# Graph attention on one core: an extra exponential placed ahead of ScalarE's block loop in each of the three attention layers

## The chip, the cores and the metric

One core of a Trainium2 chip runs the whole program in one launch. The metric is the device time of one execution in microseconds (us). The engines are TensorE (PE; PEld are its weight loads), VectorE (DVE), ScalarE (ACT), GpSimd (POOL) and the sync engine (SP); "ACTq" in a row is an instruction that ScalarE's queue issues itself, here a DMA.

## The reference, cut to what matters

Two blocks work on a graph of 3125 nodes and 53125 edges: a dot-product attention over the edges (8 heads), a mixture of experts, two graph-attention layers (4 heads), and a small gated network. All three attention layers need, for each destination node, a softmax over its neighbours:

```python
s = jnp.einsum('edh,edh->eh', q[rows], k[cols])          # attention layer
e = jnp.exp(s - m[rows])
out = segment_sum(e / z[rows] * v[cols], rows)

e = leaky_relu(alpha_s[src] + alpha_d[dst], 0.2)         # graph-attention layer, two of them
ex = jnp.exp(e - m[dst])
out = segment_sum(h[src] * (ex / segment_sum(ex, dst)[dst]), dst)
h = gelu(out + b)
```

Nothing of this changes.

## The kernel before

`program` runs its stages one after another: the edge lists are loaded and sorted into tables of neighbours, then come the attention layer (`attend`, named att, with `qk=True`), the experts, and the two graph-attention layers (`attend`, named gt0 and gt1, with `qk=False`; their tiles are called gt_... in the profile), and `finish`.

`attend` handles destination nodes in tiles of 128. The neighbours of a tile are taken in chunks, 4 rounds (one neighbour per node and round) to a chunk; four chunks, one for each of four buffer slots, make a block. A block is one turn of a hardware loop on each engine. There are 19 turns with 4 rounds (`Fori(0, full)`, the full turns) and then 9 turns with 3 rounds (`Fori(full, blocks)`, the tail turns).

- POOL (`gather_block`, L1004 to L1009) waits until a slot's last contents have been weighted and its list of indices is there, then issues 4 (in the tail 3) indirect DMAs that gather the neighbours' rows into the slot.
- DVE (`block_of`) works on slot k and the slots before it in turn: scores (L1059 or L1061, L1069 or L1071), the running maximum (L1077), the shift by it (L1082), then for slot k-1 the weighting of the gathered rows by the exponentials (`weight_chunk`, L1088 for gt, L1092 for att), and the rescaling and adding of sums (L1101, L1107).
- ACT (`weigh_block`) computes the exponential of each slot's shifted scores (L1208). In att it also weights part of the rows with 16 short copies a slot (8 in the tail, L1213), and SP hands the slots over. In gt ACT does the handing over (`hand_over`, L1192 to L1194): it waits until the gather into the slot has landed, tells DVE, reads the next list column into a register (L947) and issues the DMA of the next indices (L944). At the end of a turn it issues the load of the next list (L951).
- PE (`sum_block`, L1259) sums the weighted rows.

In a gt turn ACT's program order is: hand over slots 0 and 1, exponential of slot 0, hand over slot 2, exponential of slot 1, and so on:

```python
for k in range(SLOTS):
    if handing and k + 1 < SLOTS:
        hand_over(k + 1, at, passed)
    n = act.snap(i * SLOTS + (k + 1))
    act.wait_ge(shifted, n)
    act.activation(wv[...] if qk else exps_of(k)[...], score[:, k, 0:rounds + 1, :], ACT.Exp).then_inc(exped, 1)
```

ScalarE evaluates functions from a table, which an `ACT_TABLE_LOAD` brings in. The compiler puts those instructions in, the kernel's source has none. It put one at the head of the first exponential in the body of each layer's loop of full turns, and none in the body of the tail loop.

Of the kernel before, what the change touches and what calls it, by code (L numbers as in the profile page):

```python
# [6 lines left out]
ALU, ACT, AX = mybir.AluOpType, mybir.ActivationFunctionType, mybir.AxisListType  # L7

P = 128
# [872 lines left out]
def attend(nc, c, g, name, heads, own, own_rows, table, width, qk, bias_row=None, begin=None, onward=None):  # L882
# [22 lines left out]
    with Mem(nc, name) as m:  # L905
# [6 lines left out]
        score = m.sb("score", [P, SLOTS, ROUNDS + 1, h])  # L912
        wv = m.sb("wv", [P, SLOTS, ROUNDS + (1 if qk else 0), h, av])
        recip = m.sb("recip", [P, 2, NT, h])
        part = m.ps("part", [P, SLOTS, 512])
        exps = None if qk else m.ps("exps", [P, SLOTS, 64])
        exps_of = lambda k: exps[:, k, 0:(ROUNDS + 1) * h].rearrange("p (r h) -> p r h", h=h)
# [17 lines left out]
        def blocks_of(eng):  # L935

            full = eng.value_load(g.counts[0:1, 0:1], min_val=MIN_FULL, max_val=MAX_FULL)
            tails = eng.value_load(g.counts[0:1, 1:2], min_val=1, max_val=TAIL_ROUNDS * NT)
            full = eng.snap((full + (SLOTS - 1)) // SLOTS)
            return full, eng.snap(full + (tails + (SLOTS - 1)) // SLOTS)  # L940

        def load_idx(eng, col, k):

            eng.dma_start(idx[:, k, :], g.neighbours[:, bass.ds(col, ROUNDS)]).then_inc(idx_in[k], 16)  # L944

        def col_of(eng, at):
            return eng.value_load(listed[0:1, bass.ds(at, 1), 1], min_val=0, max_val=MAX_COLS - ROUNDS)  # L947

        def load_list(eng, i):

            eng.dma_start(listed[:, bass.ds(i % LISTS * SLOTS, SLOTS), :], g.tile_of[bass.ds(i * SLOTS, SLOTS), :].unsqueeze(0)).then_inc(list_in, 16)  # L951

        with nc.Block(no_gpsimd_drain=True) as block:
# [228 lines left out]
            @block.scalar  # L1182
            def _(act):
                act.sem_inc(act_weighted, SLOTS)
                for k in range(groups if qk else 0):
                    part_t = slice(GROUP * k, GROUP * (k + 1))
                    act.dma_start(own[:, part_t, :], own_rows[:, part_t, 0:QW]).then_inc(own_rest if k else own_in, 16)
                    act.dma_start(acc[:, part_t, :, :].rearrange("p t h f -> p t (h f)"), own_rows[:, part_t, QW:2 * QW]).then_inc(own_rest if k else own_in, 16)
                    act.dma_start(peak[:, part_t, :], own_rows[:, part_t, 2 * QW:QX]).then_inc(own_rest if k else own_in, 16)

                def hand_over(k, at, passed):
                    act.wait_ge(gathered[k], passed)  # L1192
                    act.sem_inc(chunk_ready, 1)
                    load_idx(act, col_of(act, at + k), k)  # L1194

                def weigh_block(i, rounds, passed):
                    of_act = range(dve_rounds, rounds)
                    if handing:
                        at = act.snap((i + 1) % LISTS * SLOTS)
                        act.wait_ge(list_in, i * 16 + 32)  # L1200
                        act.sem_inc(list_seen, 1)
                        hand_over(0, at, passed)
# [5 lines that stand above are left out]
                        act.activation(wv[:, k, 0:rounds + 1, :, dh] if qk else exps_of(k)[:, 0:rounds + 1, :], score[:, k, 0:rounds + 1, :], ACT.Exp).then_inc(exped, 1)  # L1208
                        if act_rounds:
                            act.wait_ge(exped, n)  # L1210
                            for r in of_act:
                                for e in range(h):
                                    last = act.activation(wv[:, k, r + 1, e, 0:dh], rows[:, k, r, v0 + e * dh:v0 + (e + 1) * dh], ACT.Copy,  # L1213
                                                          scale=wv[:, k, r + 1, e, dh:dh + 1])
                            last.then_inc(act_weighted, 1)
                    if handing:
                        load_list(act, i + 2)

                full, blocks = blocks_of(act)
                with act.Fori(0, full) as i:  # L1220
                    weigh_block(i, ROUNDS, (i + 1) * (16 * ROUNDS))
                with act.Fori(full, blocks) as i:
                    weigh_block(i, TAIL_ROUNDS, (i + 1) * (16 * TAIL_ROUNDS) + full * (16 * (ROUNDS - TAIL_ROUNDS)))
                if handing:
                    act.wait_ge(list_in, blocks * 16 + 32)
                    act.sem_inc(list_seen, 1)
                    for k in range(SLOTS):
                        act.wait_ge(idx_in[k], blocks * 16 + 16)
                        act.sem_inc(list_seen, 1)
                def copy_group(k):  # L1230
                    for t in range(GROUP * k, GROUP * (k + 1)):
                        act.wait_ge(turned, t + 1)
                        if t >= 2:
                            act.wait_ge(projected, t - 1)
                        act.activation(a_t[:, t % 2, :, :].rearrange("p h n -> p (h n)"), part[:, t % 2, 0:D], ACT.Copy).then_inc(copied, 1)

                def gelu_group(k):
                    act.wait_ge(biased, k + 1)
                    out = own[:, GROUP * k:GROUP * (k + 1), 0:D]
                    act.activation(out, out, ACT.Gelu).then_inc(gelued, 1)  # L1240

                for k in range(0 if qk else 2 if onward is not None else groups):
                    gelu_group(k)
                for k in range(groups if onward is not None else 0):
                    copy_group(k)
                    if not qk and k + 2 < groups:
                        gelu_group(k + 2)
# [820 lines left out]
def program(nc, a, out):  # L2068
# [3 lines left out]
    with Mem(nc, "all") as m:  # L2072
# [56 lines left out]
        with Mem(nc, "first") as first:  # L2129
            wo, bo = first.sb("wo", [P, KC, D]), first.sb("bo", [P, D])  # L2130
            row_f = first.sb("row_f", [P, 2, NT])
            weights_in = first.sem("weights_in")
            loads = [(wo[:, :, :], by_half(a.Wo)), (bo[:, :], one_row(a.bo).to_broadcast([P, D])), (wr[:, :, :], by_half(a.Wr)), (br[:, :], one_row(a.br).to_broadcast([P, NE])),
                     (gw[:, :, :], by_half(a.gW)), (gb[:, :], one_row(a.gb).to_broadcast([P, E2])), (x[:, :, :], x_rows)]
            late = []
            for i, (v, s_src, s_dst) in enumerate(((a.gW0, a.a_src0, a.a_dst0), (a.gW1, a.a_src1, a.a_dst1))):
                loads.append((ga[i][:, :, 0:D], by_half(v)))
                for k, s in enumerate((s_src, s_dst)):
                    for h in range(GH):
                        late.append((vectors[i][(h % 2) * GC:(h % 2 + 1) * GC, h // 2, k * GH + h:k * GH + h + 1],  # L2140
                                     s[h, :].rearrange("(c o) -> c o", o=1)))
            with Mem(nc, "at") as p:
                own = p.sb("own", [P, NT, QW])
                attend(nc, c, graphs[0], "att", QH, own, q_ordered, kv_rows, KVP, True, begin=(loads, late, vectors, weights_in),
                       onward=(wo, own, att_rows, D, bo[:, :]))
            xn_rows = dram("xn_rows", (NPAD, D))
            add_and_norm(nc, c, att_rows, graphs[1].order, row_f, out_row, wr, br, weights_in, 16 * (len(loads) + len(late)), x, logits, xn_rows)
# [9 lines left out]
        with Mem(nc, "gat") as p:  # L2157
            own = [p.sb(f"own{i}", [P, NT, TP]) for i in range(2)]
            combine_and_project(nc, c, r, g.order, y_rows.rearrange("t p f -> (t p) f"), x, ga, vectors, own, h_rows[0])
            attend(nc, c, g, "gt0", GH, own[0], None, h_rows[0], TP, False, bias_row=a.gb0, onward=(ga[1], own[1], h_rows[1], GW, None))  # L2160

            attend(nc, c, g, "gt1", GH, own[1], None, h_rows[1], TP, False, bias_row=a.gb1)
            finish(nc, c, x, own[1], gw, gb, a, out, out_row)
# [360 lines left out]
```

## Time and profile before

| what | us |
|---|---|
| median of 3 runs (lowest, highest) | 3999.95 (3995.61, 4002.75) |
| the profiled execution's own time | 3977.9 |
| its span, first to last instruction | 3976.3 |
| PE busy | 2371.0 (60%) |
| DVE busy | 2242.8 (56%) |
| POOL busy | 1653.0 (42%) |
| ACT busy | 1396.2 (35%) |

No engine is busy for the whole span, and the stages have different limits, so the shares say little about one edit; the loops that it touches have to be read by themselves, turn by turn.

### The profile page before, as it was taken

To read this page: it belongs to the slowest core of one execution; us is meant where nothing else is said; L and a number is where in the kernel's file an instruction comes from. 1 tells how busy PE (TensorE), PEld (TensorE's weight loads), DVE (VectorE), ACT (ScalarE), POOL (GpSimd) and SP (SyncE) were. 2 spreads that over 40 slices of the span, in tenths; PEclk is the share of its full clock that TensorE was granted. 3 is DMA by queue.
4 is the path that set the end of the run, shared out by engine and by line. 5 is a ranking of instruction groups with operands and counts; after the bars stand their busy time and mean duration, and the time that the engine had idled before them with its cause. 6 is when DMAs were issued, how large, how long until landed. Compare 5 with 4: busy or idle time off the path is not lost. (4 is left out here: it accounts for less than half of the span.)

```text
span 3976.3 us, 62355 instructions
## 1 busy us (share of the span) xinstructions
PE 2371.0 (60%) x14988; PEld 1705.1 (43%) x14989; DVE 2242.8 (56%) x6592; ACT 1396.2 (35%) x4027; POOL 1653.0 (42%) x1767
## 2 busy tenths in 40 slices
PE   7357852789254555645999843444445345544399
PEld 4255212732133333444999832333323233333288
DVE  7868997799476777754111144444445344445632
ACT  2636850589376774311444320000001100000144
POOL 1112202030567766530222266666654666666311
PEclk9578985899577676665999966767667776677699
DMA  4166201820866766422222123333432334443200
GB/s 166 55 152 187 77 3 39 228 77 0 252 193 196 205 189 189 128 87 61 79 78 78 41 93 103 109 106 105 105 101 76 106 106 109 112 107 107 76 16 19
DMA packets 254860, 429.06 MB, mean 108 GB/s; under 512 B 99328, under 2 KB 179758, under 8 KB 253846
## 3 DMA queue, kind: packets, MB, share of 16 engines
q0 software_dynamic: 91312, 315.99, 27.4%
q1 hardware_dynamic: 120438, 104.16, 9.4%
q10 hardware_dynamic: 42992, 7.34, 1.0%
q8 instruction: 74, 1.21, 0.1%
q14 instruction: 44, 0.36, 0.0%
HBM read 374.57 MB, written 52.77 MB: 107 GB/s over the span
## 5 line engine op out<-in xcount | busy, mean ns | idle before, releaser
L1259 PE MATMUL gt_part<-gt_wv,all_ident 128*128 128x260 f32 x1648 | 598.8, 528 | 715.9 <-DVE gt_wv L1088 612.3
L1009 POOL DMA_INDIRECT gt_rows<-h_rows,gt_idx x824 | 791.5, 961 | 491.8 <-DVE gt_wv L1088 256.7
L1259 PEld LDWEIGHTS gt_part<-gt_wv,all_ident 128*128 128x128 f32 x1648 | 417.4, 265 | 897.4 <-DVE gt_wv L1088 688.4
L1009 POOL DMA_INDIRECT att_rows<-kv_rows,att_idx x412 | 432.6, 1050 | 346.4 <-issue 159.0
L1259 PE MATMUL att_part<-att_wv,all_ident 128*128 128x264 f32 x824 | 328.8, 566 | 343.2 <-ACT att_wv L1213 166.8
L1259 PEld LDWEIGHTS att_part<-att_wv,all_ident 128*128 128x128 f32 x824 | 217.7, 279 | 453.9 <-issue 320.5
L1088 DVE TENSOR_TENSOR gt_wv<-gt_rows,gt_exps 128x1040 f32<-128x1040 f32 (+1 forms) x224 | 260.7, 1164 | 172.2 <-ACT gt_exps L1208 150.6
L1213 ACT ACTIVATE att_wv<-att_rows,att_wv 128x32 f32<-128x32 f32 x1504 | 336.4, 308 | 58.8 <-issue 38.8
L1208 ACT ACTIVATE gt_exps<-gt_score 128x20 f32<-128x20 f32 (+1 forms) x224 | 42.5, 190 | 738.1 <-issue 425.9
L1208 ACT ACT_TABLE_LOAD x57 | 73.1, 1283 | 546.6 <-issue 546.4
L1565 PE MATMUL ex_up<-ex_xe,ex_w 128*128 128x128 f32 x1760 | 207.8, 277 | 12.4 <-DVE ex_xe L1529 12.4
L1565 PEld LDWEIGHTS ex_up<-ex_xe,ex_w 128*128 128x128 f32 x1760 | 206.9, 193 | 16.3 <-DVE ex_xe L1529 12.8
L1574 PE MATMUL ex_down<-ex_w,ex_hid 128*128 128x256 f32 x880 | 199.0, 379 | 0.0
L1059 DVE TENSOR_TENSOR att_prod<-att_rows,at_own 128x1056 f32<-128x1056 f32 (+1 forms) x112 | 132.5, 1183 | 82.4 <-SPq L963 55.9
L805 PE MATMUL ixcs_window<-ixcs_oh_c,ixcs_oh_p 128*128 128x512 f16 x416 | 160.8, 416 | 29.6 <-ACT ixcs_oh_p L790 17.1
L790 ACT ACTIVATE ixcs_oh_p<-ixcs_oh_l,edges_value_of_d 128x128 f16<-128x128 f16 x416 | 161.9, 400 | 32.2 <-DVE ixcs_oh_c L732 16.0
L805 PE MATMUL ixcd_window<-ixcd_oh_c,ixcd_oh_p 128*128 128x512 f16 x416 | 160.7, 397 | 19.5 <-ACT ixcd_oh_p L790 3.9
L790 ACT ACTIVATE ixcd_oh_p<-ixcd_oh_l,edges_value_of_s 128x128 f16<-128x128 f16 x416 | 165.5, 401 | 18.2 <-DVE ixcd_oh_c L732 6.5
L1574 PEld LDWEIGHTS ex_down<-ex_w,ex_hid 128*128 128x128 f32 x880 | 162.9, 190 | 19.9
L1587 ACT ACT_TABLE_LOAD x55 | 70.6, 1283 | 274.5 <-PE ex_up L1565 274.5
L1107 DVE TENSOR_TENSOR gt_acc<-gt_acc,gt_part 128x260 f32 x224 | 95.2, 425 | 116.6 <-issue 65.0
L1529 DVE TENSOR_SCALAR ex_xe<-ex_turn,ex_ln_g,ex_ln_b 128x128 f32<-128x128 f32 x112 | 40.8, 406 | 199.5 <-PE ex_turn L1550 179.3
(540 smaller groups left out, 5112.4 us busy)
## 6 DMA issues: line engine op xcount, KB each, us to landing
ex_w<-in_W SPq DMA_DIRECT2D x16, 1024.0 KB, 7.4
ixbs_parts_bc<-key_parts_s SPq DMA_DIRECT2D x13, 1024.0 KB
ixbs_parts_bc<-key_parts_s SPq DMA_DIRECT2D x26, 512.0 KB
ixbd_parts_bc<-key_parts_d SPq DMA_DIRECT2D x13, 1024.0 KB
ixbd_parts_bc<-key_parts_d SPq DMA_DIRECT2D x26, 512.0 KB
gt_rows<-h_rows,gt_idx POOLq DMA_INDIRECT x824
kv_rows<-qk_kv_all SPq DMA_DIRECT2D x5, 1440.0 KB, 8.2
y_rows<-ex_y POOLq DMA_DIRECT2D x55, 128.0 KB, 2.0
```

The source lines that it names most:

```text
L790: act.activation(oh_p[k % RING][:, :], oh_l[k % RING][:, :], ACT.Copy, scale=values[:, bass.ds(i * BATCH + k, 1)]).then_inc(valued, 1)
L805: pe.matmul(window[:, :], oh_p[k % RING][:, :], oh_c[k % RING][:, :], start=False, stop=True, skip_group_check=True).then_inc(summed, 1)
L1009: pool.indirect_dma_start(out=rows[:, k, r, :], out_offset=None, in_=table, in_offset=bass.IndirectOffsetOnAxis(ap=idx[:, k, r:r + 1], axi ...
L1059: dve.tensor_tensor(of_row, row[:, :, 0:D + h], q, ALU.mult).then_inc(multiplied, 1)
L1088: dve.tensor_tensor(wv[:, k, 0:rounds, :, :], rows[:, k, 0:rounds, 0:HW].rearrange("p r (h f) -> p r h f", f=av), exps_of(k)[:, 1:rounds + ...
L1107: dve.tensor_tensor(a, a, part[:, k, 0:h * av], ALU.add).then_inc(added, 1)
L1208: act.activation(wv[:, k, 0:rounds + 1, :, dh] if qk else exps_of(k)[:, 0:rounds + 1, :], score[:, k, 0:rounds + 1, :], ACT.Exp).then_inc( ...
L1213: last = act.activation(wv[:, k, r + 1, e, 0:dh], rows[:, k, r, v0 + e * dh:v0 + (e + 1) * dh], ACT.Copy, scale=wv[:, k, r + 1, e, dh:dh + 1])
L1259: last = pe.matmul(part[:, k, 0:h * av], c.ident[:, :], wv[:, k, first_wv + r, :, :].rearrange("p h f -> p (h f)"), start=(r == 0), stop=( ...
L1565: last = pe.matmul(up[:, q // 2, (q % 2) * P:(q % 2 + 1) * P], w1[:, k, h, q * P:(q + 1) * P], xe[:, h, :], start=(h == 0), stop=(h == KC ...
L1574: last = pe.matmul(out, hid[:, q, :], w2[:, k, q, :], start=(q == 0), stop=(q == HC - 1))
L1587: act.activation(hid[:, q, :], up[:, q // 2, (q % 2) * P:(q % 2 + 1) * P], ACT.Gelu, bias=b1[:, bass.ds(e, 1), q]).then_inc(act_done, 1)
```

## The change

One tile of one column is added, and one exponential of it is computed on ScalarE between the reading of the loop counts and the loop of full turns. Its result is used by nothing; the semaphore `passed` that it adds to is waited for by nobody.

```diff
@@ -912,6 +912,7 @@
         recip = m.sb("recip", [P, 2, NT, h])
+        first_exp = m.sb("first_exp", [P, 1])
         part = m.ps("part", [P, SLOTS, 512])
@@ -1217,6 +1218,7 @@
                 full, blocks = blocks_of(act)
+                act.activation(first_exp[:, :], c.eps[:, :], ACT.Exp).then_inc(passed, 1)
                 with act.Fori(0, full) as i:
                     weigh_block(i, ROUNDS, (i + 1) * (16 * ROUNDS))
```

What it does to the instructions is seen in ScalarE's order. First the attention layer, from the counts to the first weighting of the loop body; before:

```order
L938 TENSOR_LOAD all_counts_s
L938 ISA x2
L1220 UNCONDITIONAL_BRANCH
L1220 ISA
L1208 ACT_TABLE_LOAD
L1208 ACTIVATE att_wv<-att_score 128x40
L1213 ACTIVATE att_wv<-att_rows,att_wv 128x32 x16
```

and with the change, where the lines behind L914 have moved down by one and those behind L1220 by two:

```order
L939 TENSOR_LOAD all_counts_s
L939 ISA x2
L1221 ACT_TABLE_LOAD
L1221 ACTIVATE att_first_exp<-all_eps 128x1
L1222 UNCONDITIONAL_BRANCH
L1222 ISA
L1209 ACTIVATE att_wv<-att_score 128x40
L1214 ACTIVATE att_wv<-att_rows,att_wv 128x32 x16
```

The branch opens the loop; the load now stands ahead of it. Second, the loop body of a graph-attention layer on ScalarE, from the second hand-over to the third; before:

```order
L944 DMA gt_idx<-neighbours_d 128x4
L1207 ISA
L1208 ACT_TABLE_LOAD
L1208 ACTIVATE gt_exps<-gt_score 128x20
L947 ISA
```

and with the change:

```order
L945 DMA gt_idx<-neighbours_d 128x4
L1208 ISA
L1209 ACTIVATE gt_exps<-gt_score 128x20
L948 ISA
```

The load is gone from the body, and nothing else in it has moved. The other engines' instructions and the rest of ScalarE's are the same in both kernels.

## Rows read from the trace of the kernel before

**Rows 1.** Costliest groups: out<-in xcount | busy us, mean ns | idle before, releaser.
```profile
L1009 POOL DMA_INDIRECT gt_rows<-h_rows,gt_idx x824 | 791.5, 961 | 491.8 <-DVE gt_wv L1088 256.7
L1208 ACT ACT_TABLE_LOAD x57 | 73.1, 1283 | 546.6 <-issue 546.4
```
**Rows 2.** The instructions of L1208 in gt0, in gt1 and in att, one window each.
```profile
L1208 ACT ACT_TABLE_LOAD  x19: 1283/1283/1283, 2410.5 to 2860.7; - x19
...
L1208 ACT ACT_TABLE_LOAD  x19: 1283/1283/1283, 3124.1 to 3563.5; - x19
...
L1208 ACT ACT_TABLE_LOAD  x19: 1283/1283/1283, 1042.7 to 1468.6; - x19
```
**Rows 3.** Timeline of one full turn of gt0: start, us, engine, line [idle before <-releaser].
```profile
2812.24 0.71 ACTq L944 DMA_DIRECT2D gt_idx<-neighbours_d  x1
2812.27 1.28 ACT L1208 ACT_TABLE_LOAD   x1 [13.90 <-issue]
2813.57 0.19 ACT L1208 ACTIVATE gt_exps<-gt_score 128x20 f32<-128x20 f32 x1
2813.79 1.24 DVE L1088 TENSOR_TENSOR gt_wv<-gt_rows,gt_exps 128x1040 f32<-128x1040 f32 x1 [4.81 <-ACT gt_exps L1208]
2815.81 0.94 POOL L1009 DMA_INDIRECT gt_rows<-h_rows,gt_idx  x1 [4.46 <-DVE gt_wv L1088]
2826.61 10.52 ACTq L944 DMA_DIRECT2D gt_idx<-neighbours_d  x2
2833.00 0.18 DVE L1061 TENSOR_TENSOR gt_prod<-gt_rows,gat_own 128x16 f32<-128x16 f32 x1 [1.18 <-issue]
2834.60 0.95 POOL L1009 DMA_INDIRECT gt_rows<-h_rows,gt_idx  x1 [0.30 <-issue]
2837.76 0.19 ACT L1208 ACTIVATE gt_exps<-gt_score 128x20 f32<-128x20 f32 x1
2840.01 0.95 POOL L1009 DMA_INDIRECT gt_rows<-h_rows,gt_idx  x1 [4.46 <-DVE gt_wv L1088]
```
**Rows 4.** Timeline of one tail turn of gt0, where no table is loaded.
```profile
2941.08 0.31 ACTq L944 DMA_DIRECT2D gt_idx<-neighbours_d  x1
2941.52 0.19 ACT L1208 ACTIVATE gt_exps<-gt_score 128x16 f32<-128x16 f32 x1 [11.46 <-issue]
2943.61 0.95 POOL L1009 DMA_INDIRECT gt_rows<-h_rows,gt_idx  x1 [4.83 <-DVE gt_wv L1088]
2954.32 6.69 ACTq L944 DMA_DIRECT2D gt_idx<-neighbours_d  x2
2957.91 0.17 DVE L1061 TENSOR_TENSOR gt_prod<-gt_rows,gat_own 128x12 f32<-128x12 f32 x1 [0.55 <-issue]
2961.14 0.19 ACT L1208 ACTIVATE gt_exps<-gt_score 128x16 f32<-128x16 f32 x1 [11.50 <-issue]
2963.23 0.95 POOL L1009 DMA_INDIRECT gt_rows<-h_rows,gt_idx  x1 [4.88 <-DVE gt_wv L1088]
```
**Rows 5.** Timeline: POOL's first gather of a turn, first and last of those counted; one load and its shift.
```profile
2470.72 0.95 POOL L1009 DMA_INDIRECT gt_rows<-h_rows,gt_idx  x1 [6.12 <-issue]
3567.07 0.95 POOL L1009 DMA_INDIRECT gt_rows<-h_rows,gt_idx  x1 [5.01 <-DVE gt_wv L1088]
...
2739.70 1.28 ACT L1208 ACT_TABLE_LOAD   x1 [13.06 <-issue]
2740.10 0.17 DVE L1082 TENSOR_TENSOR gt_score<-gt_score,gt_new_peak 128x20 f32<-128x20 f32 x1
```
**Rows 6.** Timeline of POOL around turns 7 to 13 of gt0, and 4 to 5 of gt1.
```profile
2566.74 0.94 POOL L1009 DMA_INDIRECT gt_rows<-h_rows,gt_idx  x1 [4.51 <-DVE gt_wv L1088]
2743.24 0.95 POOL L1009 DMA_INDIRECT gt_rows<-h_rows,gt_idx  x1 [7.04 <-DVE gt_wv L1088]
...
3207.41 0.95 POOL L1009 DMA_INDIRECT gt_rows<-h_rows,gt_idx  x1 [4.34 <-DVE gt_wv L1088]
3255.47 0.95 POOL L1009 DMA_INDIRECT gt_rows<-h_rows,gt_idx  x1 [4.20 <-DVE gt_wv L1088]
```
**Rows 7.** Timeline of att: the first load, one that is waited for, one that is not.
```profile
1042.70 1.28 ACT L1208 ACT_TABLE_LOAD   x1 [47.77 <-issue]
1048.60 1.22 POOL L1009 DMA_INDIRECT att_rows<-kv_rows,att_idx  x1 [27.39 <-ACT att_wv L1213]
...
1110.54 0.19 DVE L1082 TENSOR_TENSOR att_score<-att_score,att_new_peak 128x40 f32<-128x40 f32 x1
1111.56 1.28 ACT L1208 ACT_TABLE_LOAD   x1 [3.62 <-issue]
1112.86 0.27 ACT L1208 ACTIVATE att_wv<-att_score 128x40 f32<-128x40 f32 x1
1120.56 0.94 POOL L1009 DMA_INDIRECT att_rows<-kv_rows,att_idx  x1 [3.58 <-issue]
...
1202.41 1.28 ACT L1208 ACT_TABLE_LOAD   x1
1204.75 0.19 DVE L1082 TENSOR_TENSOR att_score<-att_score,att_new_peak 128x40 f32<-128x40 f32 x1
1204.98 0.27 ACT L1208 ACTIVATE att_wv<-att_score 128x40 f32<-128x40 f32 x1 [1.29 <-issue]
```

## The prediction

> **What bounds the kernel now.** I began with the costliest groups. A table load takes 1283 ns and there are 57 of them at L1208, 73.1 us in all; in the same loops POOL's gathers are idle for 491.8 us, more than half of it until DVE's weighting L1088 [rows 1]. So the loads are few, and what counts is whether anything waits for them. The view of one line, with a window for each layer, says where they are: 19 in gt0, 19 in gt1, 19 in att, one for each full turn, none in the tail turns [rows 2].
>
> Then I read the timeline of one turn and followed what released what. In gt0 the load starts at 2812.27, the first exponential of the turn follows at 2813.57, DVE's weighting at 2813.79, which had been idle for 4.81 us until that exponential, and POOL's first gather of the next turn at 2815.81, after 4.46 us of idle time until that weighting. The next such gather is at 2840.01. The turn is a closed ring of 24.20 us: POOL's gathers, ACT's hand-over of slots 0 and 1, load, exponential, weighting, POOL again [rows 3]. POOL alone would need less: the first and the last of its 16 gathers start at 2815.81 and 2834.60, 18.79 us apart in 15 steps, 1.253 each, so 16 steps are 20.0 us [rows 3]. The remaining 4.2 us of the turn are waiting. POOL is not the bound, and the load lies on the ring.
>
> What makes ACT late is not the load in the main. ACT's two index DMAs of the hand-overs are spread over 10.52 us [rows 3], and the tail turn, which has no load, has nearly the same wait of POOL, 4.83 and 4.88 us in a turn of 19.62 (2943.61 to 2963.23) [rows 4]. The profile doesn't name what holds ACT's queue there ("issue"). The change leaves it alone.
>
> **The change, part by part.** *Removed:* 54 of the 57 loads, since the loop bodies lose theirs and three stand ahead of the loops. *Added:* three exponentials of one column. The nearest row is 0.19 us for 20 columns [rows 3], so with the loads moved ahead this is 3 x (1.28 + 0.19) = 4.4 us of ACT. It costs nothing: ACT then waits for the first gathers anyway; ahead of its first load of att it is idle for 47.77 us [rows 7]. Were that cover missing, the 4.4 us would be the price. *Waits:* none is added, and nobody waits for the semaphore that the new instruction raises. No DMA is moved.
>
> *The worth of one load in gt.* From the load's start to the exponential are 1.30 us (2812.27 to 2813.57) [rows 3]. Two other distances bound it, both against the tail turn, which is this loop without a load. From ACT's index DMA to the exponential the full turn needs 1.33 us and the tail turn 0.44 (2941.08 to 2941.52), so 0.89 would be won: the load began while the queue was still at its DMA, and part of it may be cover for that. From DVE's L1061 of slot 1 (which ACT's hand-over releases) to the exponential the full turn needs 4.76 us (2833.00 to 2837.76) and the tail turn 3.23 (2957.91 to 2961.14), so 1.53 would be won [rows 3, 4]. I take 1.30, the directly measured one, and keep 0.89 and 1.53 as ends.
>
> *How many of the 38 turns in gt.* I went through all of them. In 28 (14 in each layer) POOL waited for over 2 us ahead of its first gather of the next turn; the first of them ended at 2470.72 and the last at 3567.07 [rows 5]. In 23 of these the shift of the scores (L1082) was done before the load began, so the whole 1.29 to 1.30 us are exposed: 29.7 us. In the other five the shift came after the load's start: as where the load starts at 2739.70 and the shift starts at 2740.10 and takes 0.17 [rows 5], and what is exposed is 1.04, 1.18, 0.72, 0.66 and 0.65 us, 4.3 in all. Sum for gt: 34 us. The other 10 turns, mostly turns 0, 1 and 7 to 12, have their wait at another slot, where the load is at best one cause of several. I put them at nothing, with 10 x 1.30 = 13 us as the other end.
>
> *att.* ACT is busier there (16 copies after each exponential). In most turns the load runs while ACT would be waiting for DVE anyway: load at 1202.41, shift at 1204.75, exponential at 1204.98, nothing lost. In turn 0 the load is the last thing ahead of all of it (load at 1042.70, POOL's wait of 27.39 us ended at 1048.60), and in turns 3, 16 and 18 the shift was done before and POOL waited afterwards: as with the shift at 1110.54, load at 1111.56, exponential at 1112.86, POOL's wait of 3.58 us ahead of 1120.56 [rows 7]. That is 4 x 1.3 = 5 us, with 0 and 8 as ends.
>
> *What is late next.* With the load gone, ACT's hand-over of slot 1 is followed by the exponential at once. POOL's wait falls from 4.46 to about 3.2 us, and is still a wait for L1088, with ACT's queue behind it; POOL's own 20.0 us are still below the turn's 22.9.
>
> *The sum.* 34 + 5 = 39 us. The profiled execution took 3977.9 us, so 3938.9 for its like. The median of the runs is 3999.95, 22 us above it; I carry the difference over unchanged: 3999.95 - 39 = **3961 us**. With the ends (28 x 0.89 = 25; 28 x 1.53 + 13 + 8 = 64) the gain is 25 to 64, the time 3936 to 3975. Changes under 0.2%, 8 us, I call no difference; a measurement of this kernel can tell no less.
>
> The rows price a load at 1.28 us and show no other instruction in front of it. The Trainium skill, ScalarE: Activation LUTs, section What ACT_TABLE_LOAD costs, gives the same 1283 ns and adds a drain of about 1380 ns, 2.66 us for a switch to a different set. By that the sum would be 32 x 2.66 = 85 us, an estimate from that page.
>
> **The rivals.**
>
> *A. The queue in front of the load empties the engine as well*, so a load costs more than its own row. With a second stretch as long as the load, 32 exposed loads give 32 x 2 x 1.28 = 82 us: 3918. For it speaks only that the 0.89 and the 1.53 us differ, so something around the load is not seen. Against it: the load starts 0.03 us after the start of the DMA ahead of it, and in the fully exposed turns nothing but 0.02 us lies between load and exponential [rows 3]. The page named above states that drain for a change of set; from the second turn on these loads bring in the set that is there already. 0.04.
>
> *B. All turns profit*, the ten irregular ones and 1.5 us each: a gain of 50 to 64 us, time about 3943. 0.10.
>
> *C. Part of it is taken back.* ACT's queue is slow in a stretch of each turn (10.52 us for two hand-overs, 6.69 in the tail) [rows 3, 4]. If that stretch ends at its own time, by when the gathers end, an exponential that could start earlier is held by it in half of the turns: gain 10 to 25, time about 3982. 0.09.
>
> *D. No difference.* If that slow stretch were a property of the profiled execution alone, the turns of the timed runs would be POOL's 20.0 us and the loads hidden. Against it: then the timed runs would be shorter than the profiled one by some 38 x 4.2 = 160 us, and they are 22 us longer. Or the exponential waits for something else that ends with the load by chance; against that stand the 23 turns with the same 1.29 to 1.30. Time 3992 to 4008. 0.11. That the loads stay in the bodies is excluded by ScalarE's order, in which they stand ahead of the loops.
>
> *E. Slower: the regular turns break up.* The ring repeats at 24.2 us because ACT's slow stretch falls ahead of the turn's first exponential. In turns 7 to 13 of gt0 it doesn't: POOL's gathers at 2566.74 and 2743.24 are 7 turns apart, 176.5 us or 25.2 each [rows 6], against 24.2. If the earlier exponential pushes the slow stretch behind itself, the load's time is lost again at a later slot and the 28 regular turns take 25.2: 28 x 1.0 = 28 us more, less the 5 of att: 3999.95 + 23 = 4023. It decides from the point where a shift of 1.3 us puts the slow stretch on the other side of the exponential. Against it: in gt1 the ring takes 24.0 (3207.41 to 3255.47, two turns) [rows 6] and recovers from its own irregular turns, and the tail turns, which are this loop without a load, are as regular as the full ones [rows 4]. 0.05.
>
> **How the numbers follow.** The forecast, 3961 with 3949 to 3975 as its own range, has 0.61. Faster: 0.61 + 0.04 + 0.10 + 0.09 = 0.84. Same: D, 0.11. Slower: E, 0.05. The range starts at 3938, within B, and ends at 4000, in the middle of D. Left out are A (0.04), E (0.05), half of D (0.055) and a part of B (0.04): 0.185.
>
> **What would show it in the profile after.** ACT_TABLE_LOAD in the line of the new exponential, x3, and none at the loop's exponential. In gt0's regular turns: ACT's exponential within 0.5 us of the index DMA; POOL's idle time ahead of the first gather 3.2 us instead of 4.46, still released by L1088; a turn of 22.9 us instead of 24.2; tail turns unchanged at 19.6. POOL's idle time in its gt gathers down by some 30 us, DVE's and PE's busy times unchanged. In att a span shorter by about 5 us. The prediction is wrong if the regular turns keep 24.2 us, with the 1.3 us found again in front of the exponential or at another slot (C, D), if they stop being regular (E), or if the wait falls by over 2 us a turn (A).

## The result, and the profile of the changed kernel

The changed kernel takes 4020.88 us (median of 14 runs, 4002.47 to 4025.32). The kernel before, run beside it, takes 3996.06 (14 runs, 3979.79 to 4004.53). The ratio is 1.0065, 95% interval 1.0051 to 1.0078: slower, with the medians 24.8 us apart, where 39 us of gain were forecast. The profiled execution took 4024.9 us, near its median, while that of the kernel before (3977.9) lies 18 us under its own. So the two profiles differ by 47 us, and differences read from them overstate the loss.

The loads went where they should. One line of the changed kernel, L1221, with everything that it issues (count, duration in ns, first and last start):

```profile
L1221 ACT ACT_TABLE_LOAD  x3: 1283/1283/1283, 1042.8 to 3125.6; - x3
L1221 ACT ACTIVATE gt_first_exp<-all_eps x2: 203/203/203, 2401.5 to 3126.9; 128x1 f32<-128x1 f32 x2
L1221 ACT ACTIVATE att_first_exp<-all_eps x1: 203/203/203, 1044.1 to 1044.1; 128x1 f32<-128x1 f32 x1
```

ACT's busy time fell by 65.6 us, nearly the 69.3 us of 54 loads of 1.283. None of it shortened the kernel. From the page of the changed kernel, busy time first, then POOL's gathers in the gt layers:

```profile
PE 2319.3 (58%) x14988; PEld 1673.2 (42%) x14989; DVE 2238.5 (56%) x6592; ACT 1330.6 (33%) x3976; POOL 1649.9 (41%) x1767
...
L1010 POOL DMA_INDIRECT gt_rows<-h_rows,gt_idx x824 | 790.4, 959 | 541.5 <-DVE gt_wv L1089 288.7
```

POOL's gathers cost what they did, but they wait for 541.5 us, where it had been 491.8 [rows 1]. That is 49.7 us more instead of some 30 less. The next view is POOL's gathers in gt0 and in gt1, one window each (count, ns, first and last start); the changed kernel:

```profile
L1010 POOL DMA_INDIRECT gt_rows<-h_rows,gt_idx x412: 941/947/6228, 2401.5 to 3061.0; - x138
...
L1010 POOL DMA_INDIRECT gt_rows<-h_rows,gt_idx x412: 941/947/6228, 3126.6 to 3788.6; - x138
```

and the kernel before:

```profile
L1009 POOL DMA_INDIRECT gt_rows<-h_rows,gt_idx x412: 943/949/6056, 2392.4 to 3035.8; - x138
...
L1009 POOL DMA_INDIRECT gt_rows<-h_rows,gt_idx x412: 943/949/6101, 3106.0 to 3735.1; - x138
```

gt0 went from 643.4 to 659.5 us and gt1 from 629.1 to 662.0: 49.0 us in the two. What happened inside a turn is seen in ScalarE's timeline of the changed kernel (start, us, engine, line [idle before <-releaser]):

```profile
2800.87 1.60 ACTq L945 DMA_DIRECT2D gt_idx<-neighbours_d  x2
2802.78 0.19 ACT L1209 ACTIVATE gt_exps<-gt_score 128x20 f32<-128x20 f32 x1 [5.20 <-DVE gt_score L1083]
...
2805.96 0.19 ACT L1209 ACTIVATE gt_exps<-gt_score 128x20 f32<-128x20 f32 x1 [2.99 <-issue]
...
2810.03 0.19 ACT L1209 ACTIVATE gt_exps<-gt_score 128x20 f32<-128x20 f32 x1 [3.88 <-issue]
2824.01 0.19 ACT L1209 ACTIVATE gt_exps<-gt_score 128x20 f32<-128x20 f32 x1 [13.79 <-issue]
...
2827.52 1.60 ACTq L945 DMA_DIRECT2D gt_idx<-neighbours_d  x2
2829.40 0.19 ACT L1209 ACTIVATE gt_exps<-gt_score 128x20 f32<-128x20 f32 x1 [5.20 <-DVE gt_score L1083]
```

Compare it with [rows 3]. There the two index DMAs of the hand-overs were spread over 10.52 us; here they need 1.60. There ScalarE's long wait (13.90 us) stood ahead of load and exponential 0; here a wait of 13.79 us stands between exponential 2 and exponential 3. The slow stretch is still in the turn, but it has changed sides: it no longer falls on ScalarE's hand-overs. What it did to them before is seen in the instructions that ScalarE's queue runs for a hand-over, at the line that reads the list column (count, ns lowest/median/highest). First the turn of [rows 3] in the kernel before, 2826 to 2838 us; then the turn above; then a gt loop of a run that took 3632 us (gt alone on occasion 3634, told below), 2290 to 2700 us:

```profile
L947 ACTq FUSED_REGOPS  x3: 170/697/708, 2826.0 to 2831.5; - x3
...
L948 ACTq FUSED_REGOPS  x7: 64/152/170, 2803.3 to 2828.4; - x7
...
L948 ACTq FUSED_REGOPS  x161: 64/144/171, 2299.4 to 2699.7; - x161
```

In the slow stretch a register instruction of ScalarE's queue takes some 700 ns; outside of it, and throughout the last run's window, it takes 64 to 171. In the changed kernel's turn the stretch hits DVE's wait for PE. PE's, DVE's and POOL's rows of the same turn:

```profile
2807.69 2.02 PE L1261 MATMUL gt_part<-gt_wv,all_ident 128*128 128x260 f32 x8 [0.68 <-issue]
...
2823.46 0.42 DVE L1108 TENSOR_TENSOR gt_acc<-gt_acc,gt_part 128x260 f32 x1 [11.45 <-DMA qkv_x_all<-in_x]
...
2828.69 0.94 POOL L1010 DMA_INDIRECT gt_rows<-h_rows,gt_idx  x1 [6.92 <-DVE gt_wv L1089]
```

DVE stands for 11.45 us ahead of adding a slot's sum. (The releaser named there, a DMA of another stage, was long done; L1108 waits for PE's sum of slot 1.) By PE's rows that sum was done at 2809.71, so it isn't PE's work that is slow; what holds the signal back the profile doesn't show. All that follows is late, and POOL's wait is now 6.92 us, at another slot of the turn. The turn, exponential 0 to exponential 0, is 26.62 us here.

In both turns the engine that was held goes on at about the time when POOL's gathers end. POOL's last gather before its wait ended at 2811.35 in [rows 3] (2815.81 less 4.46) and the load started at 2812.27, 0.92 us later; here it ended at 2821.77 and L1108 started at 2823.46, 1.69 us later. POOL then waits for whatever is left to do from there. In [rows 3] that is load, exponential 0 and weighting; here it is L1108, the shift, exponential 3, the next turn's first hand-over and the weighting of slot 3, 5.23 us from L1108 to POOL. That the gathers cause the stretch isn't shown: on the faster occasions told below POOL issues without a break and no stretch is there.

### The profile page after: what moved, and what is told of

Read it like the earlier page. It is cut to its first block and busy times, and to the rows that moved or that the text cites. A ratio compares the mean times of both kernels' runs of the same rounds, so it can differ in the third digit from the quotient of the medians.

```text
span 4023.2 us, 62304 instructions
## 1 busy us (share of the span) xinstructions
PE 2319.3 (58%) x14988; PEld 1673.2 (42%) x14989; DVE 2238.5 (56%) x6592; ACT 1330.6 (33%) x3976; POOL 1649.9 (41%) x1767
## 5 line engine op out<-in xcount | busy, mean ns | idle before, releaser
L1261 PE MATMUL gt_part<-gt_wv,all_ident 128*128 128x260 f32 x1648 | 557.6, 499 | 797.2 <-DVE gt_wv L1089 618.3
L1010 POOL DMA_INDIRECT gt_rows<-h_rows,gt_idx x824 | 790.4, 959 | 541.5 <-DVE gt_wv L1089 288.7
L1261 PEld LDWEIGHTS gt_part<-gt_wv,all_ident 128*128 128x128 f32 x1648 | 390.6, 249 | 964.3 <-DVE gt_wv L1089 668.9
L1108 DVE TENSOR_TENSOR gt_acc<-gt_acc,gt_part 128x260 f32 x224 | 95.1, 424 | 358.2 <-DMA qkv_x_all<-in_x 180.4
L732 DVE TENSOR_SCALAR ixcd_oh_c<-all_iota_h,ixd_place 128x512 f16<-128x512 f16 x416 | 152.7, 367 | 0.3 <-PE ixcd_window L805 0.3
```

What stands on the lines that cost most here:

```text
L732: dve.tensor_scalar(oh_c[k % RING][:, :], c.iota_h[:, :], at_tile(i * BATCH + k, 0), None, ALU.is_equal).then_inc(made, 1)
L1010: pool.indirect_dma_start(out=rows[:, k, r, :], out_offset=None, in_=table, in_offset=bass.IndirectOffsetOnAxis(ap=idx[:, k, r:r + 1], axi ...
L1108: dve.tensor_tensor(a, a, part[:, k, 0:h * av], ALU.add).then_inc(added, 1)
L1261: last = pe.matmul(part[:, k, 0:h * av], c.ident[:, :], wv[:, k, first_wv + r, :, :].rearrange("p h f -> p (h f)"), start=(r == 0), stop=( ...
```

## The experiments

The timed runs of each kernel alternate with runs of the kernel before on the same chip; I call one such group of runs an occasion and name it by the time that the kernel before took on it. The names exponential 0 to 3 are those of a turn's four slots.

**Occasion 3634: the first four.** *Copy ahead*: the added instruction as a Copy, so that all loads stay in the bodies.

```diff
-                act.activation(first_exp[:, :], c.eps[:, :], ACT.Exp).then_inc(passed, 1)
+                act.activation(first_exp[:, :], c.eps[:, :], ACT.Copy).then_inc(passed, 1)
```

> The instruction ahead of the loop is a copy, not an exponential; every table holds the copy, so the load should stay in the body of the loop of full turns (57 loads at the loop's exponential) and only one instruction ahead of the loop is added. Phase theory (the load held the turn's first exponential back by 1.3 us, and without it the slow stretch falls behind it): as before, ratio 0.998 to 1.002. Rival, layout of the code (one instruction more ahead of the loop shifts where the loop body lies in ScalarE's instruction stream): slower like the change, 1.004 to 1.009.

*Long copy* and *short copy*: the change, and in full turns a copy in the load's place, of 1320 columns (1302 ns) or of one (some 0.2 us).

```diff
# cut: the line that makes the tile hold and the semaphore held; broadcast of iota_f
                         n = act.snap(i * SLOTS + (k + 1))
+                        if rounds == ROUNDS and k == 0:
+                            act.activation(hold[:, :, :], c.iota_f[:, 0:440]..., ACT.Copy).then_inc(held, 1)
```

> The change, and in each full turn, where the load stood, a copy of 1320 columns into a tile that nothing reads, about as long as the load (1.3 us by the kernel's 400-column copies). Phase theory: the time of before comes back, ratio 0.997 to 1.003, gt turns of 24.2 us in the regular stretches, POOL waiting ahead of its first gather. Rival, the loads themselves or fewer instructions: stays slower, 1.004 to 1.009.

> The change, and in each full turn a copy of one column where the load stood, about 0.2 us: as many instructions in ScalarE's loop as before, but not their time. Phase theory: slow like the change, 1.004 to 1.009, turns of 25 us or more. Rival, number or place of the instructions: back to 1.000.

*gt alone*: the exponential ahead of the loop only `if not qk`, so that att keeps its loads.

> The exponential ahead of the loop in gt0 and gt1 alone; att as before with its 19 loads. By the profiles att lost 13 us (first to last gather 647.5 to 660.6), gt0 16 (643.4 to 659.5) and gt1 33 (629.1 to 661.9). Phase theory: two thirds or more of the loss stay, ratio 1.004 to 1.007, since ACT hands over the slots only in gt. Rival, att is where it is lost: 1.000 to 1.002.

Measured: 0.9999 (0.9990 to 1.0007), 1.0008 (0.9999 to 1.0016), 1.0001 (0.9992 to 1.0010) and 1.0000 (0.9989 to 1.0011). None differs. The expectations were written for a kernel before of 3996 us, and the losses expected of the short copy and of gt alone didn't come. The kernel before took 3633.76 us here (35 runs). The gt layers of gt alone, POOL's gathers as above:

```profile
L1010 POOL DMA_INDIRECT gt_rows<-h_rows,gt_idx x412: 941/946/6034, 2287.5 to 2811.2; - x138
...
L1010 POOL DMA_INDIRECT gt_rows<-h_rows,gt_idx x412: 940/946/6011, 2875.0 to 3398.7; - x138
```

524 us a layer instead of 643. And the timeline of a turn of Copy ahead, with the load in it; the two rows of POOL are 16 gathers apart:

```profile
2481.19 3.64 ACTq L945 DMA_DIRECT2D gt_idx<-neighbours_d  x2
...
2484.43 0.95 POOL L1010 DMA_INDIRECT gt_rows<-h_rows,gt_idx  x1 [0.30 <-issue]
...
2484.93 1.28 ACT L1209 ACT_TABLE_LOAD   x1 [7.40 <-issue]
...
2486.22 0.19 ACT L1209 ACTIVATE gt_exps<-gt_score 128x20 f32<-128x20 f32 x1
...
2504.45 0.95 POOL L1010 DMA_INDIRECT gt_rows<-h_rows,gt_idx  x1 [0.30 <-issue]
```

There are no slow stretches. The turn is POOL's own 20.02 us, POOL waits for nothing, and the load of 1.28 us is exposed to nobody. So these four say that the loads are free where POOL is the bound, and nothing on what happened in the measurement.

**Occasion 3977: the change again.**

> The change itself, once more. In the four runs so far the kernel before took 3634 us and not 3996, and its trace shows no slow stretch: the gt turns are POOL's 20.0 us. Theory (what the change gains or loses is decided by the slow stretches alone, since without them POOL is the bound of the gt turn and the load is hidden): where the kernel before takes 3634, the ratio is 0.998 to 1.002 and the regular gt turns are 20.0 us; where it takes 3996, 1.004 to 1.009. Rival (the change loses time by itself, whatever the chip's state): 1.005 or more on both.

Measured 1.0019 (1.0008 to 1.0030). The stretches were back, the loss only in part: below the 1.004 to 1.009 that was expected with stretches.

**Occasion 3980: the change, both copies, and att alone** (the exponential ahead only `if qk`).

> The change itself, as the anchor of the three beside it. Two kinds of chip have been met: one on which the kernel before takes 3634 us and its gt turns are POOL's 20.0 us (no slow stretches), and one on which it takes 3977 to 3996 us with turns of 24 to 25 us. First kind: every theory expects 1.000. Second kind: phase theory (the slow stretch falls on the other side of the exponential, regular turns of 25.2 to 26.6 us instead of 24.2) expects 1.002 to 1.008; the prediction's theory (28 of 38 gt turns lose the load) expected 0.990; noise theory (the two measurements differ from 1 by the chip's state alone) expects 0.998 to 1.002.

> The change, with a copy of 1320 columns (about 1.3 us, no table load) at the place in ScalarE's full turns where the load stood. Phase theory: the time between ScalarE's hand-overs and exponential 0 is what it was before, so the ratio goes back to 0.998 to 1.002 on a chip with slow stretches. Rival, that the loads themselves or the one early exponential matter otherwise (code layout, the table's state): the ratio stays where the change alone is, 1.002 to 1.008. On a chip without slow stretches 1.000 by both.

> The same copy with one column (about 0.2 us): the same instructions as the kernel before it, but not their duration. Phase theory: within 0.002 of the change alone (1.002 to 1.008), and above the long copy. If the number of instructions in the loop mattered and not their time, long and short copy would agree within 0.001. On a chip without slow stretches 1.000.

> The exponential ahead of the loop in att layers alone; the gt layers keep their loads. Both theories put most of the difference into the two gt layers (34.9 us of the first measurement's profiled runs, against 10.4 in att): expected 0.999 to 1.003 on a chip with slow stretches, 1.000 on one without.

Measured: change 1.0008 (0.9993 to 1.0023), long copy 1.0006 (0.9993 to 1.0019), short copy 1.0004 (0.9989 to 1.0018), att alone 0.9969 (0.9958 to 0.9980). Long and short copy agree with the change and with each other. As the change itself differs from the kernel before by no more than the noise here, these times can't tell whether the long copy brings the old time back; the turns, counted below, say that it doesn't bring the old turns back. And the long copy was no true stand-in for a load. In the trace of that kernel it began where the queue had not yet issued the last index DMA, as here:

```profile
2733.76 1.30 ACT L1210 ACTIVATE gt_hold<-all_iota_f 128x1320 f16<-128x1320 f32 x1 [5.34 <-issue]
2734.73 0.01 ACTq L946 DMA_DIRECT2D gt_idx<-neighbours_d  x1
2736.09 0.19 ACT L1212 ACTIVATE gt_exps<-gt_score 128x20 f32<-128x20 f32 x1 [1.03 <-issue]
```

The copy was over 1.03 us before the exponential started, so it lay in a wait. What this occasion does show is the split: att alone (eight runs) is faster by 0.3%, with the gt loads left in; with those removed too, that is gone. Its 0.9969 lies below the 0.999 to 1.003 expected.

**Occasion 3989: gt alone and Copy ahead.** They ran first on an occasion at 3630, with att alone and the change beside them.

> The exponential ahead of the loop in gt layers alone. Theory of the locked turn: with the load in the body a gt layer's full turns settle on one length, 24.1 to 24.2 us, for half of its turns (9 to 10 of 18 in every gt layer profiled so far with loads); without the load they don't settle and average 24.7 to 25.5. So slower than before, 1.002 to 1.006 on a chip with slow stretches, and no more than 3 turns in a row of 24.1 to 24.2 us in its profile. Prediction's theory: 0.991. Theory that the gt loads are hidden: 1.000 plus or minus 0.0015. On a chip without slow stretches (before at 3634) 1.000 by all.

> The exponential ahead in att alone, a second time. It was 0.9969 on one chip. Theory of the locked turn: gt layers settle as before, att gains a little, 0.996 to 0.999, and its profile has 4 or more turns in a row of 24.1 to 24.2 us in each gt layer. If the first measurement was the chip's noise: 0.9985 to 1.0015. On a chip without slow stretches 1.000.

> A Copy ahead of the loop where the change has an Exp: the one added instruction, and every load still in the body. Both theories: 0.999 to 1.001, and gt turns that settle on 24.1 to 24.2 us. A value of 1.002 or more would say that the added instruction or the code's place matters and not the loads.

> The change, beside its two halves. If the halves add up, its ratio is the product of those of att alone and gt alone within 0.001: about 0.997 times 1.004, 1.000 to 1.003. Three measurements of it on chips with slow stretches gave 1.0065, 1.0019 and 1.0008.

Measured, in this order: 1.0000, 0.9995, 1.0003, 1.0004, with intervals that all hold 1. Without slow stretches nothing could be told. The second time they were there, with the kernel before at 3989.14 us.

> The exponential ahead in gt layers alone, again, in the hope of a chip with slow stretches (before at 3970 to 4000 us). There: theory of the locked turn 1.002 to 1.006, and never more than 3 turns in a row of 24.1 to 24.2 us in its profile; prediction's theory 0.991; hidden loads 1.000 plus or minus 0.0015. On a chip with before at 3630 us: 1.000.

> The Copy ahead, loads in the body, again. On a chip with slow stretches 0.999 to 1.001 and gt turns that settle on 24.1 to 24.2 us for 7 or more of 18; 1.002 or more, or no settled turns, would say that the added instruction matters by itself. On a chip with before at 3630 us: 1.000.

Measured: gt alone 1.0073 (1.0054 to 1.0092), 4022.07 us in six runs, above the 1.002 to 1.006 expected; Copy ahead 1.0007 (0.9990 to 1.0024), 3992.17, as expected. The added instruction by itself costs nothing that can be measured; the loss is in the gt layers. POOL's gathers by layer, gt alone first:

```profile
L1010 POOL DMA_INDIRECT gt_rows<-h_rows,gt_idx x412: 941/947/6087, 2405.6 to 3061.6; - x138
...
L1010 POOL DMA_INDIRECT gt_rows<-h_rows,gt_idx x412: 941/947/6022, 3127.5 to 3782.0; - x138
```

Copy ahead:

```profile
L1010 POOL DMA_INDIRECT gt_rows<-h_rows,gt_idx x412: 941/947/6127, 2402.1 to 3039.0; - x138
...
L1010 POOL DMA_INDIRECT gt_rows<-h_rows,gt_idx x412: 941/947/6133, 3109.0 to 3751.4; - x138
```

656.0 + 654.5 us against 636.9 + 642.4: 31.2 us. The medians are 29.9 apart and the two profiled executions 34.9, so nearly the whole difference between the two kernels lies there.

How the turns differ is seen where both have the slow stretch on the same side, ahead of exponential 3. ScalarE's rows of one such turn of Copy ahead, with POOL's row that has the wait:

```profile
2471.94 1.59 ACTq L945 DMA_DIRECT2D gt_idx<-neighbours_d  x2
2473.64 1.28 ACT L1209 ACT_TABLE_LOAD   x1 [5.49 <-issue]
...
2474.93 0.19 ACT L1209 ACTIVATE gt_exps<-gt_score 128x20 f32<-128x20 f32 x1
...
2492.26 0.19 ACT L1209 ACTIVATE gt_exps<-gt_score 128x20 f32<-128x20 f32 x1 [11.04 <-issue]
...
2497.32 0.94 POOL L1010 DMA_INDIRECT gt_rows<-h_rows,gt_idx  x1 [4.50 <-DVE gt_wv L1089]
...
2499.12 0.19 ACT L1209 ACTIVATE gt_exps<-gt_score 128x20 f32<-128x20 f32 x1
```

and of gt alone:

```profile
2476.32 1.60 ACTq L945 DMA_DIRECT2D gt_idx<-neighbours_d  x2
2478.22 0.19 ACT L1209 ACTIVATE gt_exps<-gt_score 128x20 f32<-128x20 f32 x1 [5.30 <-DVE gt_score L1083]
...
2498.73 0.19 ACT L1209 ACTIVATE gt_exps<-gt_score 128x20 f32<-128x20 f32 x1 [13.09 <-issue]
...
2503.51 0.94 POOL L1010 DMA_INDIRECT gt_rows<-h_rows,gt_idx  x1 [6.30 <-DVE gt_wv L1089]
...
2504.23 0.19 ACT L1209 ACTIVATE gt_exps<-gt_score 128x20 f32<-128x20 f32 x1 [5.31 <-DVE gt_score L1083]
```

From exponential 3 to the next exponential 0 it is 6.86 us with the load and 5.50 without: the 1.3 us that were forecast are there. From exponential 0 to exponential 3 it is 17.33 with and 20.51 without. The turn has lost 3.18 us behind the exponential for 1.36 won ahead of it, 26.01 against 24.19 us, and POOL waits for 6.30 us instead of 4.50. The pair is a wide one: the means of such turns in these two profiles are 25.21 and 24.65 us (next table).

**All gt turns of nine profiles.** I took 34 turns of each (turns 1 to 17 of gt0 and of gt1, exponential 0 to exponential 0, from the timelines) and sorted them. Form A: the four exponentials within 9.7 us, the long wait ahead of exponential 0, as in [rows 3]. Form B: exponentials 0 to 2 within 8.2 us, and over 6 us until exponential 3. The number of turns of each form, with their mean length in us:

| kernel, occasion | gt loads in body | form A | form B | other | mean of all |
|---|---|---|---|---|---|
| before, profile of 3977.9 us | yes | 24, 23.55 | 6, 26.20 | 4 | 24.5 |
| Copy ahead, 3989 | yes | 25, 24.11 | 6, 24.65 | 3 | 24.6 |
| att alone, 3980 | yes | 22, 23.67 | 5, 27.87 | 7 | 24.8 |
| change, 3996 | no | 0 | 29, 25.38 | 5 | 25.5 |
| gt alone, 3989 | no | 0 | 34, 25.21 | 0 | 25.3 |
| change, 3977 | no | 7, 22.43 | 7, 27.21 | 20 | 24.7 |
| change, 3980 | no | 9, 23.05 | 18, 26.15 | 7 | 25.0 |
| short copy, 3980 | no | 9, 22.86 | 15, 25.64 | 10 | 24.6 |
| long copy, 3980 | no | 8, 21.99 | 7, 26.88 | 19 | 25.1 |

(The last column is of all full turns but the first, by POOL's first gathers.) With the loads in the gt bodies, 22 to 25 of 34 turns have form A, in each of three profiles, and up to seven of them follow one another at 24.0 to 24.3 us. The form doesn't fix the length: Copy ahead has five turns of form B in a row at 24.2 us. Without the loads form A has 9 turns at most, and no more than two in a row have such a length. Where form A does occur without a load, it is shorter, as forecast: 22.0 to 23.05 in the mean, against 23.55 to 24.11. (These means mix more than the load: the lowest is that of the long copy.) On occasion 3980 the last column doesn't order the kernels as their times do: att alone, the faster one, has 24.8 us, and the change 25.0. So the forms are shown as what goes with the load, and the size of a loss can't be worked out from them. The timeline of the change on occasion 3980, exponentials 0 and POOL's rows with a wait:

```profile
2709.47 0.19 ACT L1209 ACTIVATE gt_exps<-gt_score 128x20 f32<-128x20 f32 x1 [11.83 <-DVE gt_score L1083]
...
2711.94 0.94 POOL L1010 DMA_INDIRECT gt_rows<-h_rows,gt_idx  x1 [4.96 <-DVE gt_wv L1089]
...
2732.55 0.19 ACT L1209 ACTIVATE gt_exps<-gt_score 128x20 f32<-128x20 f32 x1 [13.87 <-issue]
...
2734.80 0.94 POOL L1010 DMA_INDIRECT gt_rows<-h_rows,gt_idx  x1 [3.16 <-DVE gt_wv L1089]
...
2756.43 0.95 POOL L1010 DMA_INDIRECT gt_rows<-h_rows,gt_idx  x1 [6.93 <-DVE gt_wv L1089]
...
2757.13 0.19 ACT L1209 ACTIVATE gt_exps<-gt_score 128x20 f32<-128x20 f32 x1 [5.21 <-DVE gt_score L1083]
```

From POOL's first gather to the next turn's are 22.86 us (2711.94 to 2734.80), with a wait of 3.16: the forecast's 22.9 and 3.2. POOL's last gather had ended at 2731.64 and exponential 0 started 0.91 us later, just where the load stood in [rows 3]. But the turn ahead of this one had taken 28.3 us, and the next turn is of form B: POOL's wait is 6.93 us, at slot 3, and exponential 0 to exponential 0 takes 24.58 us.

**What the load does that a copy doesn't** was to be told by the change with the long copy and, behind it, a wait of ScalarE's queue for the copy's end, `act.wait_ge(held, i + 1)`, in both kinds of layer and then in gt alone; att alone was to be measured again.

> The change, with the 1320-column copy in the load's place and behind it a wait of ScalarE's queue for the copy's end, so that the queue stands still for those 1.3 us as it does during a load (with the copy alone it ran on: the copy of one turn started 2.3 us ahead of its exponential). On a chip with slow stretches: if what settles the turn is that the queue is held between hand-over 1 and exponential 0, gt turns settle again on 24.1 to 24.3 us for 7 or more of 18, and the ratio is 0.998 to 1.002. If it is something else about the load, no settled turns, mean gt turn 24.7 to 25.5 us, and 1.001 to 1.008 as for the change. On a chip with before at 3630 us: 1.000 by both.

> The exponential ahead in att layers alone, the version that measured 0.9969, for which a second measurement on a chip with slow stretches is still missing. If the att loads are worth something there: 0.996 to 0.999. If that was the chip and the day: 0.999 to 1.002. In both cases 4 or more gt turns in a row of 24.1 to 24.2 us. On a chip with before at 3630 us: 1.000.

> The change in both kinds of layer, and in the gt loops' full turns the 1320-column copy with the queue's wait for its end. On a chip with slow stretches: if the held queue is what settles the turns, 7 or more of 18 turns of each gt layer have 24.1 to 24.3 us, and the ratio is that of att alone, 0.996 to 1.001. If not, no settled turns, mean gt turn 24.7 to 25.5 us, and 1.001 to 1.008 as for the change. On a chip with before at 3630 us: 1.000 by both.

The runs fell on occasions at 3632 and 3629 us and gave 1.0003 (0.9991 to 1.0015), 1.0004 (0.9994 to 1.0015) and 1.0005 (0.9995 to 1.0015). Without slow stretches they tell nothing of this, and the question stays open.

## Why the prediction was wrong

**Right: what the loads are and where they go.** 54 loads left the bodies and three stand ahead. A load is exposed for its 1.28 us in turns of form A, and such a turn without it is shorter by that much (22.9 us in the turn shown). Rival A, twice the price, is out for that turn: 24.2 less 22.9 leaves room for the load alone. The Trainium skill, ScalarE: Activation LUTs, section What ACT_TABLE_LOAD costs, has a drain on top for a switch to a different set; the loads of the loops bring in the set that is there. Switches are in every run too, in `finish`, between the tables of the square root and of the exponential. One of them in the kernel before:

```profile
3814.65 0.88 ACT L1937 ACTIVATE f_h<-f_p,f_bias 128x128 f32<-128x128 f32 x3 [0.39 <-PE f_p L1858]
3815.55 1.28 ACT L1911 ACT_TABLE_LOAD   x1
3816.85 0.22 ACT L1911 ACTIVATE f_gates<-f_raw 128x20 f32<-128x20 f32 x1
```

The activation ahead ends 0.02 us before the load, and the next starts 1.30 us after the load's start. So this trace doesn't agree with the Trainium skill: a switch takes the load's 1.3 us here, and no drain stands ahead of it or behind it.

**Wrong: the step "What is late next".** It let the exponential move forward by 1.3 us and kept everything else in the turn in its place, with ACT's slow queue still what POOL's wait hangs on. That made 28 turns with a wait of 3.2 us instead of 4.46, 34 us in all. The slow stretch is not tied to ScalarE's queue: it moved behind exponential 0, where it holds DVE ahead of L1108, and the path from there to POOL is the longer one (POOL's waits at slot 3 have a median of 5.6 us in the changed kernel's full turns, and 6.92 in the turn shown). In the profile of the changed kernel no turn kept form A, so that the number 28 became 0, and the mean full turn in gt went from 24.5 to 25.5 us.

**Rival E had it, at a chance of 0.05.** It gave 4023 us by 25.2 us a turn; measured were 4020.9, and turns of 25.4. That the total fits so well is partly luck: E's 28 us for gt less 5 for att are not the parts that the profiles show (49 and 13 us more, against a profile of the kernel before that was short by 18). What I held against it was no evidence: that gt1 found back to its regular turns showed how stable they are with the load in the ring, and the regular tail turns are another loop with fewer gathers (12, not 16). The kernel before had shown turns of other kinds in ten places, some of them in [rows 6]; I had put them at nothing because the load was not on their path, when they showed that the ring has a second way to run. E's point of decision, as I had put it, isn't whole either: Copy ahead has turns with the stretch behind exponential 0 that take 24.2 us, while the kernel before and att alone, with the load too, have means of 26.20 and 27.87 us for such turns. What sets their length isn't shown.

**Rival C had part of it:** ScalarE goes on when the gathers end. But that doesn't hold the earlier exponential back in the turn of form A shown: it starts 0.91 us behind POOL's last gather, as the load did before (0.92).

**The size depends on the occasion.** The change measured 1.0065, 1.0019, 1.0008 and, without slow stretches, 1.0004 (0.9995 to 1.0012). Nowhere was it a gain. Of rival D half is true: the stretches are no property of the profiled execution, since profile and timed runs agree within 0.6% on every occasion; but it is true that without them the turn is POOL's 20.0 us and the loads are hidden.

**att** was put at 5 us of gain. In the first two traces its gathers span 13 us more with the change, but Copy ahead and gt alone, which both keep att's loads, have such long att layers on occasion 3989 as well (660 and 662 us), so the change isn't what made it long. att alone is 8.3 us faster by the medians on the one occasion with slow stretches where it ran, 0.9969 (0.9958 to 0.9980). That agrees in sign, but its profiled execution (3984.9 us) was 12.7 us above its median and shows no shorter att layer (651.1 us, first to last gather, where the change has 645.1 on that occasion), so where the gain lies isn't shown, and it hasn't been repeated with stretches. It is the only version here that beat both kernels, on that occasion alone.

**Open:** what makes the slow stretch; why a ring with the load keeps form A and one without doesn't; and why an occasion keeps part of form A (3977, 3980) or none (3996, 3989).

## What to carry to other kernels

The ring of engines here, with some slack and a disturbance in each turn, had more than one way to run. An edit that shortens one link of such a ring can move the disturbance on to another engine, so price it with the other kind of turn that the trace already shows, and give that case a real chance. And look at the time of the kernel before on each occasion first: whether a small edit can matter at all was decided there.

## What the runs showed of the hardware that I had not expected

The kernel before took 3976.99, 3980.47, 3989.14 and 3996.06 us on four occasions and 3633.76, 3629.98, 3631.97 and 3628.67 on four others, about 9% less, and within an occasion it never changed over. It is not a fixed property of a chip, as far as the chip's number tells: the same number gave 3976.99 and 3631.97 us. The two kinds differ in the gather loops in the first place. att's gathers, first to last start, in the kernel before (first row) and in gt alone on occasion 3634 (second fence):

```profile
L1009 POOL DMA_INDIRECT att_rows<-kv_rows,att_idx x412: 943/949/2012, 1001.4 to 1648.9; - x138
```

```profile
L1010 POOL DMA_INDIRECT att_rows<-kv_rows,att_idx x412: 940/946/1638, 999.8 to 1577.5; - x138
```

The 1000 us ahead of the first gather are the same within 2 us; the layer takes 647.5 us in the one and 577.7 in the other, and each gt layer 629 to 643 against 524. The gathers themselves are not slower (medians 949 and 946 ns); what is missing in the faster kind is the stretch in each turn in which the queues and the sums are held: in gt alone on occasion 3634 the queue's register instructions at L948 take 171 ns at most, where in a slow stretch they take some 700.
